# Retention scores: stacked 96-row operands replaced by four row tiles of 32 rows, one head each

## What is computed

```python
qr = theta_shift(q, sin_q, cos_q)                    # q = xf @ Wq.T, 8 heads of 32
kr = theta_shift(k, sin_k[None, None], cos_k[None, None])
qk = jnp.einsum('bhqd,bhkd->bhqk', qr, kr) * mask[None]
den = jnp.clip(jax.lax.stop_gradient(jnp.abs(qk)).sum(-1, keepdims=True), 1.0, 50000.0)
qk = qk / den
out = jnp.einsum('bhqk,bhkd->bhqd', qk, vr).transpose(0, 2, 1, 3)
out = (out - mu) / jnp.sqrt(var + LN_EPS) * ln_g + ln_b      # per head
out = jax.nn.gelu(out.reshape(B, L, H * HD), approximate=False) @ Wo.T
```

## Time and profile before

| | us |
|---|---|
| median of 3 runs (2480.19 to 2482.9) | 2480.55 |
| profiled execution, its own time | 2480.11 |
| its span | 2478.3 |
| layer 0, first to last product of the trace | about 30.7 to 1020 |

### The profile page before, as it was taken

One profiled execution on the slowest core, in us unless ns is written; L12 is line 12 of the kernel. 1 busy time (PEld: TensorE's weight loads), 2 busy tenths in 40 slices (PEclk: granted clock), 3 DMA queues, 4 the chain that ended last, 5 costly groups with the idle time before them and its releaser, 6 DMA issues.

```text
span 2478.3 us, 36390 instructions
## 1 busy us (share of the span) xinstructions
PE 2433.9 (98%) x13326; PEld 1685.6 (68%) x13326; DVE 1849.5 (75%) x2772; ACT 1464.6 (59%) x2063; POOL 1001.1 (40%) x695
## 2 busy tenths in 40 slices
PE   8999999999999999999999899999999999999999
PEld 4444444444444444699899778888888888888887
DVE  5888888888888888777777567777666667777775
ACT  3676767676767676666666455555554555555554
POOL 3787777777777777323331301111111100111110
PEclk9999999999999999999999999999999999999999
DMA  7232323232323233244554340000000000000000
GB/s 251 52 79 66 88 66 88 67 87 67 87 68 86 69 86 92 68 66 98 67 92 82 52 111 26 26 26 26 26 26 26 26 26 26 17 17 19 26 26 17
DMA packets 117057, 149.91 MB, mean 60 GB/s; under 512 B 32768, under 2 KB 74120, under 8 KB 116624
## 3 DMA queue, kind: packets, MB, share of 16 engines
q1 hardware_dynamic: 116352, 146.87, 23.4%
q10 hardware_dynamic: 528, 0.72, 0.1%
HBM read 71.93 MB, written 25.26 MB: 39 GB/s over the span
## 4 chain that ended last, share of the span: by engine, by line
PE 88%; DVE 6%; issue 2%; DMA 1%; ACT 1%; POOL 1%; SPq 0%; DVEq 0%; another core or an unknown queue 0%; POOLq 0%; ACTq 0%
PE scores L445 10%; PE scores L1763 9%; PE scores L1764 9%; PE scores L1765 9%; PE pairC L458 8%; PE pairC L475 6%; PE pairD L379 3%; DVE l_prod L586 3%; PE pairC L1763 2%; PE pairC L1764 2%; PE pairC L1765 2%; PE pairD L1763 2%; PE pairD L1764 2%; PE pairD L1765 2%; PE pairD L388 2%; PE pairD L428 2%
## 5 line engine op out<-in xcount | busy, mean ns | idle before, releaser
L586 DVE TENSOR_TENSOR l_prod<-scores,l_window 128x1024 f32<-128x1024 f32 x512 | 613.4, 1217 | 141.7 <-PE scores L445 133.6
L799 ACT ACTIVATE l_absp<-l_prod 128x1024 f32<-128x1024 f32 x512 | 540.1, 1056 | 291.8 <-DVE l_prod L586 282.1
L445 PE MATMUL scores<-l_qst,l_kst 96*128 96x512 f32 x1024 | 381.0, 463 | 12.1 <-DVE l_prod L586 9.2
L1922 ACT ACTIVATE e_r<-scores,e_bn,e_rs 128x512 f32<-128x512 f32 x256 | 197.9, 779 | 276.6 <-PE scores L1765 276.5
L2153 POOL TENSOR_TENSOR e_xnorm<-e_res,e_scale 128x1024 f32<-128x1024 f32 x16 | 39.0, 2435 | 790.6 <-DMA e_res<-t2T_scratch 790.6
L445 PEld LDWEIGHTS scores<-l_qst,l_kst 96*128 96x128 f32 x1024 | 165.0, 190 | 271.3 <-issue 131.8
L915 POOL TENSOR_TENSOR l_absp<-l_absp,l_absp 128x1024 f32<-128x1024 f32 x126 | 297.9, 2385 | 13.7 <-ACT l_absp L799 13.3
L2029 DVE CAST e_h1hi<-e_r 128x512 fp32r<-128x512 f32 x256 | 144.2, 563 | 210.3 <-ACT e_r L1922 210.1
L1932 ACT ACTIVATE e_r<-scores,e_bn,e_rs 128x512 f32<-128x512 f32 x250 | 195.0, 781 | 138.2 <-PE scores L1765 136.7
L458 PE MATMUL pairC<-l_prod,l_v 128*32 128x512 f32 x2048 | 268.1, 595 | 0.5 <-ACT l_tA L803 0.5
L2056 DVE TENSOR_TENSOR e_r<-e_r,e_wbc 128x512 f32<-128x512 f32 x250 | 170.9, 690 | 86.4 <-ACT e_r L1932 86.2
(11 more groups left out here) (249 smaller groups left out, 4975.3 us busy)
## 6 DMA issues: line engine op xcount, KB each, us to landing
l_kst<-l_hi SPq DMA_DIRECT2D x248, 64.0 KB, 2.0
l_qst<-l_hi SPq DMA_DIRECT2D x248, 64.0 KB, 2.0
l_xo<-in_x SPq DMA_DIRECT2D x32, 256.0 KB, 3.0
x_scratch<-l_xo SPq DMA_DIRECT2D x32, 256.0 KB, 2.4
l_xa<-x_scratch SPq DMA_DIRECT2D x8, 1024.0 KB, 8.2
l_xr<-x_scratch SPq DMA_DIRECT2D x8, 1024.0 KB, 5.6
t2T_scratch<-l_xt SPq DMA_DIRECT2D x8, 1024.0 KB, 14.7
e_scale<-rows_scratch SPq DMA_DIRECT2D x16, 512.0 KB, 4.1
```

The lines of the kernel that those rows point to most:

```text
L445: mm = nc.tensor.matmul(sc[j][:, s, :], kst[g][0:96, h, 128 * kt:128 * kt + 128], qst[c][0:96, h, :], start=True, stop=True)
L586: nc.vector.tensor_tensor(prod[2 * (S % 2) + j][:], sc[j][:], win[:, 4 * g + 2 * j:4 * g + 2 * j + 2, w0:w0 + QC], ALU.mult).then_inc(prod ...
L799: nc.scalar.activation(absp[S % ABS][j][:], prod[2 * (S % 2) + j][:], ACT.Abs).then_inc(abs_ready, 1)
L1922: nc.scalar.activation(r1[:, m, :], p1[m], ACT.Relu, bias=bn_[0][1][:, m, n:n + 1], scale=rs[0][:, m, n:n + 1]).then_inc(r1_ready, 1)
```

## The change

`scores` loses its second argument. One call computes all four heads of the step by 12 matmuls of 32 contraction rows each: three rounds (high k with high q, low k with high q, high k with low q), and in each round one matmul for each head, on the rows where that head lies, which are four different row tiles of the array. The three rounds add up in PSUM. The call stands ahead of the side task, waits for both products of the step before, and raises `scores_ready` once. VectorE's two products of a step stand next to each other and wait for that one count; its side work comes behind both. `kst`, `qst`, `hi`, `lo`, their semaphores and all DMAs that filled them are gone: `high` and `low` write straight into `khi`, `klo`, `qhi`, `qlo`.

```diff
-        def scores(S, j):
+        def scores(S):
 
             P, kt = S // KT, S % KT
             g, c = P // 2 % 2, P % 2
-            if kt == 0 and j == 0:
-                pe.wait_ge(q_stacked, STACK * (P + 1))
-            if c == 0 and kt % 4 == 0 and j == 0:
-                pe.wait_ge(k_stacked[kt // 4], STACK * (P // 2 + 1))
+            if P == 0 and kt == 0:
+                pe.wait_ge(first_lo, Q0 + 1)
+            elif P == 0 and kt == 4:
+                pe.wait_ge(first_lo, K1 + 1)
+            elif kt == 0:
+                pe.wait_ge(lo_ready, prep_q(P - 1) + 1)
+            elif kt == 4 and c == 0:
+                pe.wait_ge(lo_ready, prep_k(P - 1) + 1)
             if S > 0:
-                pe.wait_ge(prod_ready, 2 * S + j - 1)
-            for s in range(2):
-                h = 2 * j + s
-                mm = nc.tensor.matmul(sc[j][:, s, :], kst[g][0:96, h, 128 * kt:128 * kt + 128], qst[c][0:96, h, :],
-                                      start=True, stop=True)
+                pe.wait_ge(prod_ready, 2 * S)
+            for n, (k, q) in enumerate(((khi, qhi), (klo, qhi), (khi, qlo))):
+                for h in range(4):
+                    rows = slice(32 * h, 32 * h + 32)
+                    mm = nc.tensor.matmul(sc[h // 2][:, h % 2, :], k[g][rows, 128 * kt:128 * kt + 128], q[c][rows, :],
+                                          start=(n == 0), stop=(n == 2))
             mm.then_inc(scores_ready, 1)
...
         for S in range(KT * PHASES):
             for part in range(2):
-                if S + 1 < KT * PHASES:
-                    scores(S + 1, part)
+                if S + 1 < KT * PHASES and part == 0:
+                    scores(S + 1)
                 side_tasks(S // KT, S % KT, part)
...
-            dve.wait_ge(scores_ready, 2 * S + j + 1)
+            dve.wait_ge(scores_ready, S + 1)
...
             products(S, 0)
+            products(S, 1)
             if kt == 3 and P > 0:
                 centre(P - 1)
             if kt == 4 and P > 0:
...
             if kt == 7 and p == 0 and stats_next:
                 statistics(b + 1, (1,))
-            products(S, 1)
...
-        def high(n, stacks, count):
-
-            if stacks is not None:
-                act.wait_ge(stacks, count)
+        def high(n):
+
             act.wait_ge(sum_ready, n + 1)
-            nc.scalar.activation(hi[:], t1[:], ACT.Copy).then_inc(hi_ready, 1)
+            nc.scalar.activation(prepared(n)[0], t1[:], ACT.Copy).then_inc(hi_ready, 1)
...
-        def low(n, stacks, count):
-
-            if stacks is not None:
-                pool.wait_ge(stacks, count)
+        def low(n):
+
             pool.wait_ge(hi_ready, n + 1)
-            nc.gpsimd.tensor_tensor(lo[:], t1[:], hi[:].bitcast(F32), ALU.subtract).then_inc(lo_ready, 1)
+            high, low = prepared(n)
+            nc.gpsimd.tensor_tensor(low, t1[:], high.bitcast(F32), ALU.subtract).then_inc(lo_ready, 1)
...
+    def prepared(n):
+
+        if n % 2 == 0:
+            c = (n // 2 + 1) % 2
+            return qhi[c][:], qlo[c][:]
+        P = n // 2
+        g, part = (P // 2 + 1) % 2, slice(QC * (P % 2), QC * (P % 2) + QC)
+        return khi[g][:, part], klo[g][:, part]
```

## The result

The changed kernel takes **2501.9 us** (median of 4 runs, 2491.89 to 2504.87), the kernel before 2480.37 in the same comparison. The ratio is 1.0074, with a 95% interval of 1.0056 to 1.0093: slower by 21.5 us. A second comparison gave 1.0081 (1.0067 to 1.0096). Slower was forecast, at 2488; the time lies in the range, but the loss is more than twice the forecast's 8. The profiled execution, 2491.89 us, is the shortest of the four, so its trace shows only about half of the loss.

What follows compares the result with a forecast made beforehand. TensorE, in use for 98% of the span, was taken to bound the kernel. Seven images at +11.7 us and the first at -3.4 gave +8.3 on 2480.11, so 2488 us, range 2460 to 2545.

Steps and rivals of the forecast that it cites:

- The bound before: Layer 0 before the change: TensorE bounds kind 0 phases (30.38 us worked out, 30.42 taken); VectorE adds 1.0 in kind 3.
- Scores in three rounds of one stream: Scores on TensorE: each round of four row tiles costs one matmul, three rounds 0.69 to 0.70 us, saving 0.23 a step.
- Rival B: Score matmuls: the row tiles' weight loads go one after another, +0.75 us a step, 2670 us in all; chance 0.09.
- Rival D: Score matmuls aren't tiled and run one after another, 2.8 us against 0.69, 2970 us in all; chance 0.03.
- The further change of tiling: Between row-tiled scores and the full-array side task, in seven steps of a phase: a new cost of 0.21 us.
- Rival A: Side task behind scores: the new change of tiling is free, saving 0.55 us a phase, 2470 us in all; chance 0.20.
- The floor and the intervals: Steps of layer 0: two products then scores take at least 3.40 us; an image costs +1.6 to 1.7 us.
- The DMAs: Removing stack DMAs: no gain in steady state; at the start, first scores -2.0 us and first phase -2.7 us.
- The 30.2 for the first phase: First phase of layer 0: 30.2 us by the intervals instead of 32.94, assuming full clock comes back as early.
- The last two phases: Final phases of layer 0, 30 and 31: charged like other phases, some 1.5 us in sum.
- The last sign that the prediction named for being wrong: Where TensorE now idles, mostly steps 6 to 7: the half-speed clock coming back would make the prediction wrong; no size given.
- The sum: Whole kernel: +11.7 us over seven images and -3.4 for the first image, +8.3 us in all.

Runs made afterwards that it cites:

- two_rounds: Changed kernel without the round of low k with high q, 8 score matmuls a step instead of 12: 2475.53 us.
- dumped_stacks: Changed kernel with the 12 stack DMAs for each q and k put back after the start, into a tile nobody reads: 2500.07 us, 1.0076.
- before_head: Kernel before, with step 0's scores by row tiles without waiting for the first q stack, and next image's DMA ahead of the mask's second half: 2483.65 us, 1.0001.
- after_again: The changed kernel, unaltered, run again: 2503.02 us.
- joined_stacks: Kernel before, stacks and 96-row matmuls kept, with one scores call for four heads ahead of the side task and adjacent products: 2527.67 us, 1.018.
- filled_start: Changed kernel with three blank matmuls at each of kt = 4 and 5 of phases 0 to 3: 2497.82 us, 1.0064.
- row_halves: Changed kernel with scores split into two halves of two heads around half the side task, each with its own wait: 2641.55 us, single execution.

## Why the prediction was right, and where it was too small

*The bound before.* Right: in the trace of before TensorE is in use for all 30.42 us of a phase of kind 0 and for 29.13 of the 29.67 of kind 3. In the changed kernel the work taken from TensorE came back as the change of tiling and the floor, so kind 0 gained nothing, and the joined wait cost most in kind 3, which had the most slack: 29.67 to 30.65.

*Scores in three rounds of one stream.* Right: 0.90 and 0.97 for 0.89 and 0.96, 0.23 a round by `two_rounds`. Rival B, the loads one after another, falls on the loads themselves. The first of the weight loads of one set of scores in the changed kernel:

```profile
506.56 0.19 PEld L412 LDWEIGHTS scores<-l_qhi,l_khi 32*128 32x128 f32 x4 [0.84 <-DVE l_prod L552]
```

Four loads of 128 columns are over in 0.19 us, and a single one takes 181 to 184 ns. Rival D, no tiling at all, would have needed 2.8 us for the 12 matmuls and is out by the 0.90.

*The further change of tiling.* Right in kind: 0.15 to 0.20 where I had taken 0.21. Rival A, the one on the faster side, falls. The Trainium skill ("TensorEngine Tiling (Array Packing)", Key Properties) says that a change of tiling mode drains TensorE. The trace agrees as far as such a change costs 0.15 to 0.20 between row tiles and full array too. Whether that is a drain or a weight load that can't run ahead, no run here separates.

*The floor and the intervals.* 3.43 for 3.40. Kinds 0 to 3 took 30.87, 31.22, 32.93 and 30.65 for 30.87, 31.25, 33.05 and 30.73. An image costs 1.42 us more, for 1.6 to 1.7. The interval of the clip was 4.77 for 4.93.

*The DMAs.* Right in steady state, shown by `dumped_stacks`. At the start the steps were right (-1.8 and -2.4 in the trace for -2.0 and -2.7). The 30.2 for the first phase needs one more term than its working names: without the clip, k's projection binds from step 4 to 5, 4.67 in the trace instead of 3.65. The three phases behind it cost 2.5 us more than before instead of the 1.3 forecast. And the term is doubtful as a gain in time: in `before_head` the same 4 us came back as a half-speed stretch one phase later, and in `after_again` too; the two other traces of the changed kernel keep them. I had named the assumption, that full clock comes back as early, and should have priced it at 0 to -4.7.

*The last two phases.* This is the term of the sum that failed. I charged them like others, some 1.5 us in sum, and they cost 6.3. They have no k or v to prepare, so TensorE's own work is lighter there and the old kernel ran 3.2 us a step, 22.5 us for the seven steps of phase 31; under the floor of 3.43 and with 4.73 where VectorE's clip stands (3.55 before), they take 25.3. `joined_stacks` shows a like loss, 8 us, so it is the joined wait's. In phase 30 nearly all lies between steps 5 and 6: 4.00 us before, 6.98 now, and 5.33 in `filled_start`, whose phase 30 is the same work at full clock. The last sign that the prediction named for being wrong, a half-speed clock where TensorE now idles, came true there.

*Luck in the sum.* The sum was 8.3 us over the trace of before, and the first trace of the changed kernel has 11.6. That they are so near is in part luck: the last image cost 7.2 for 1.7 and the first image gained 1.7 for 3.4, but six images cost 8.5 for 10.0, and behind layer 0, which the forecast left alone, this one execution was 2.4 shorter by chance.

*The execution that was traced.* The median lies 10 us above that trace, which has a mean granted clock of 0.997, the highest of the eleven executions on record; their mean is 0.9932. The traced executions average 2497.6 and 2481.9, 15.6 apart, where the medians are 19 to 21.5 apart. The three traces of the changed kernel hold 23 us at half speed in the mean, and a mean clock of 0.9932 stands for 34. By 1.9 us for each 0.001 of clock, which is 5 us at half speed, that is some 4 us more. At the same clock, 0.994, lines through the eleven executions and through the 51 of the kernel before with a clock on record are 19 us apart. So most of the 4 to 6 us between traces and medians is, by this estimate, half-speed stretches that the traced executions were spared; where they lie no trace shows.

So the loss of 19 to 21 us stands as: joining the wait +44, shown; row tiles in place of stacks -25 under that wait, shown in total and as 0.21 us of the floor; VectorE's order and the DMAs in steady state 0, shown. The 25 hold what the start is worth, which is 0 in the median of the old kernel, shown, and open on the new one, where one trace of three loses it.

## What to carry to other kernels

Before you merge two waits into one, sum the loop that they form (here two products plus one set of scores, 3.43 us) and compare it with each step in turn, the lightest first and the program's last phases above all. Here the four heads of one stream fill all four banks of the scores, so taking them together gives up the second buffer, and halving the group as `row_halves` does wins nothing back, since with a side task between the halves a round costs one stream for two tiles as for four. Two halves that stand next to each other, each with its own wait, cost 0.92 together in that trace; a kernel that puts the side task behind both in every step is the obvious next one and wasn't measured. And a microsecond saved ahead of a lightly loaded stretch of TensorE isn't saved until the granted clock of the next phases has been read, in more than one execution.

## What the runs showed of the hardware

- Four row tiles of 32 rows, into four banks, stream 512 columns each in 0.23 us a round, loads of 128 columns included. A round of two costs the same (0.90 for three) when other work follows it.
- Two groups of row tiles that use different rows and banks and stand next to each other in the program run side by side: six rounds of two took 0.92 us.
- A change from row tiles to the full array costs 0.15 to 0.20 us, seen on transposes (0.59 for 0.44), projections (1.91 for 1.72) and v (1.98 for 1.78).
- DMA traffic of 50 GB/s more inside SBUF changed the busy time of TensorE by 0.04 us in 800 and that of VectorE by 0.01.
- The same program has its half-speed stretches in other places in other executions: in three traces of the changed kernel layer 0's first 130 us held none, three and none. The one behind TensorE's idle 2.46 us at 989 was there each time, yet in `filled_start` the same work behind idle 2.44 ran at full clock.
